# Decays of a selective scan in an SBUF ring of four instead of three PSUM banks

## The reference

```
delta = softplus(d_raw @ dt_proj_w + dt_proj_b)
A = -exp(A_log)
dA  = exp(delta[..., None] * A)                       # the decays
dBx = (delta * xc)[..., None] * Bm[:, :, None, :]     # what is injected
h = dA_t * h + dBx_t                                  # for each token t
y = einsum('bdn,bn->bd', h, c_t)                      # summed over the 16 states
```

## Time and profile before

| what | us |
|---|---|
| median of 3 runs | 1376.31 |
| lowest and highest | 1374.37, 1383.9 |
| profiled execution, first to last instruction | 1379.8 |
| eight scan phases (first to last scan of a batch), together | 480.37 |
| the other stretches behind the first scan, together | 770.85 |

### The profile page before, as it was taken

How to read it: one execution, slowest core, us unless ns; L and a number is a source line. 1 busy time by engine, 2 the same in 40 slices (tenths; PEclk the granted TensorE clock), 3 DMA queues, 4 the chain that set the end, 5 groups by cost and what they waited for, 6 DMA issues and landing times. The chain is left out here.

```text
span 1379.8 us, 19465 instructions
## 1 busy us (share of the span) xinstructions
PE 1207.2 (87%) x6560; PEld 760.5 (55%) x6560; DVE 1037.0 (75%) x2381; ACT 852.2 (62%) x1600; POOL 489.3 (35%) x309
## 2 busy tenths in 40 slices
PE   5974689989998889989999889989899899889698
PEld 3651145655665556555656456655656556555456
DVE  3666977599866997589866997579975998569822
ACT  2634446488646966489565866479664876469332
POOL 0103930078002950069100960049300870029300
PEclk8995579999999999999999999999999999999899
DMA  7101100030001200020001200021000300011000
GB/s 245 70 16 64 60 8 1 16 108 16 16 17 55 69 12 6 16 92 31 17 9 43 88 1 17 16 78 47 16 1 16 109 16 9 1 64 60 8 1 8
DMA packets 18514, 53.22 MB, mean 39 GB/s; under 512 B 4976, under 2 KB 5864, under 8 KB 18032
## 3 DMA queue, kind: packets, MB, share of 16 engines
q1 hardware_dynamic: 16112, 43.40, 9.8%
q0 software_dynamic: 1296, 4.20, 1.0%
q10 hardware_dynamic: 1008, 4.38, 0.8%
HBM read 45.40 MB, written 2.38 MB: 35 GB/s over the span
## 5 line engine op out<-in xcount | busy, mean ns | idle before, releaser
L1482 DVE TENSOR_TENSOR_SCAN probs_T<-bank,probs_T 128x512 f32<-128x512 f32 x256 | 303.9, 1212 | 16.1 <-ACT bank L1078 12.1
L618 PEld LDWEIGHTS bank<-w_w,hidden 128*128 128x128 f32 x2048 | 248.8, 192 | 72.9 <-issue 66.8
L602 PE MATMUL bank<-hT,w_w 128*128 128x512 f32 x512 | 262.9, 629 | 27.1 <-ACT hidden L933 26.2
L447 POOL TENSOR_TENSOR probs_T<-step_space,probs_T 128x1024 f32<-128x1024 f32 x120 | 282.2, 2358 | 5.9 <-DVE probs_T L1482 5.7
L618 PE MATMUL bank<-w_w,hidden 128*128 128x128 f32 x2048 | 251.6, 276 | 2.1 <-DVE expert_sum L1174 1.6
L933 ACT ACTIVATE hidden<-bank,w_b 128x512 f32<-128x512 f32 x256 | 169.6, 686 | 117.5 <-PE bank L602 116.9
L1006 ACT ACTIVATE probs<-bank,row_neg 128x128 f32<-128x128 f32 (+3 forms) x256 | 134.8, 528 | 151.7 <-DVE row_neg L1335 134.8
L1078 ACT ACTIVATE bank<-step_space,a_neg 128x512 f32<-128x512 f32 x256 | 167.8, 683 | 55.0 <-DVE probs_T L1482 36.7
L701 PE MATMUL bank<-k_pad,q_lat 128*128 128x512 f32 (+3 forms) x512 | 185.3, 448 | 5.8 <-DMA k_pad<-xc 5.8
L1335 DVE TENSOR_REDUCE row_neg<-bank 128x1 f32<-128x128 f32 (+3 forms) x256 | 123.5, 487 | 85.1 <-PE bank L703 82.7
L602 PEld LDWEIGHTS bank<-hT,w_w 128*128 128x128 f32 x512 | 89.0, 194 | 153.0 <-ACT hidden L933 97.0
(11 more groups left out here) (183 smaller groups left out, 1577.6 us busy)
## 6 DMA issues: line engine op xcount, KB each, us to landing
probs_T<-b_rows_dram SPq DMA_DIRECT2D x64, 512.0 KB, 3.7
w_w<-in_w_dram ACTq DMA_DIRECT2D x2, 2048.0 KB, 14.0
k_pad<-xc SPq DMA_DIRECT2D x64, 64.0 KB, 2.0
x_in<-in_x_dram POOLq DMA_DIRECT2D x8, 256.0 KB, 3.3
gate<-gate_rows_dram SPq DMA_DIRECT2D x1, 2048.0 KB, 7.0
out_dram<-x_out POOLq DMA_DIRECT2D x7, 256.0 KB, 2.8
step_space<-in_wmod_dram SPq DMA_DIRECT2D x1, 768.0 KB, 5.6
probs_T<-in_wqT_dram SPq DMA_DIRECT2D x1, 512.0 KB, 4.1
```

The costliest lines, as they stand in the source:

```text
L447: ins = nc.gpsimd.tensor_tensor(inject[:, n % 3, :, :], u[:], row.unsqueeze(1).to_broadcast([P, DH, T]), ALU.mult)
L602: mm(hid1_bank(n)[:], w["w1"][:, n // C1, n % C1 * P:(n % C1 + 1) * P], hT[3][:], start=True, stop=True).then_inc(hid1_mm.sem, 1)
L618: ins = mm(to[:, t * P:(t + 1) * P], hidden[:, (e * C1 + c) % (2 * C1), t * P:(t + 1) * P], w["w2"][:, e * C1 + c, :], start=(c == 0), sto ...
L1482: v.tensor_tensor_scan(state[:, n % 2, c, :], decay(DH * n + c)[:], inject[:, n % 3, c, :], 0.0, ALU.mult, ALU.add).then_inc(st_ok.sem, 1)
```

## The change

The decays go to a new SBUF tensor decay_ring with four slots of 128 x 512 (8 KB in each partition). ScalarE waits for scan k - 4 in place of k - 3. The scan takes its first input from the ring. To make room in SBUF the scratch of the dynamic transfers is set to 4096 bytes. Banks 4, 5 and 0 are no longer written by ScalarE during the scan. No instruction is added, removed or moved on any engine.

```diff
+        decay_ring = sb("decay_ring", [P, 4, T])
...
-        DECAY_BANK = (4, 5, 0)
...
         def decay(k):
 
-            return bank[DECAY_BANK[k % 3]]
+            return decay_ring[:, k % 4, :]
...
                 def decays(k):
-                    if k >= 3:
-                        act.wait_ge(st_ok.sem, st_ok.at(b, k - 2))
+                    if k >= 4:
+                        act.wait_ge(st_ok.sem, st_ok.at(b, k - 3))
                     n, c = divmod(k, DH)
-                    f(decay(k)[:], delta[:, c, :], ACT.Exp, scale=a_neg[:, c, n:n + 1]).then_inc(dec_ok.sem, 1)
+                    f(decay(k), delta[:, c, :], ACT.Exp, scale=a_neg[:, c, n:n + 1]).then_inc(dec_ok.sem, 1)
...
-                        v.tensor_tensor_scan(state[:, n % 2, c, :], decay(DH * n + c)[:], inject[:, n % 3, c, :], 0.0,
+                        v.tensor_tensor_scan(state[:, n % 2, c, :], decay(DH * n + c), inject[:, n % 3, c, :], 0.0,
                                              ALU.mult, ALU.add).then_inc(st_ok.sem, 1)
...
-    nc = bacc.Bacc("TRN2", target_bir_lowering=False, num_devices=1)
+    nc = bacc.Bacc("TRN2", target_bir_lowering=False, num_devices=1, dynamic_dma_scratch_size=4096)
```

## The result

| | before | after |
|---|---|---|
| median, us | 1377.55 (4 runs) | 1573.97 (4 runs) |
| lowest and highest, us | 1374.37, 1383.9 | 1566.92, 1576.36 |
| profiled span, us | 1379.8 | 1574.6 |
| eight scan phases together, us | 480.37 | 675.42 |

The ratio after to before is 1.1416, with a 95% interval of 1.1376 to 1.1456: 14% slower. The forecast was 1592 (range 1550 to 1660).

A forecast was written before the change was run, and what follows sets the result against it. VectorE was taken to bound the scan phases, with a fixed chain between them. Eight phases of 87 us against 480.37 us add 215.6 to 1379.8, giving 1595.4, or 1592 us on the median; range 1550 to 1660.

The forecast's parts named there:

- Phases add one for one, the rest is a fixed chain: Eight scan phases, 480.37 us together: longer phases lengthen the total equally; stretches between them stay near 97.8 us.
- Full exclusion, in either order, for a scan too: A scan with two SBUF inputs and a GpSimd product or sum each wait for the other's whole instruction: +215.6 us.
- The sum: Turn-taking scans, products and sums per phase: bare 83.3 us, taken as 87; eight phases add 215.6 us.
- the surcharge: Per scan phase, 87 us taken over 83.3, for scans in a row and turns sometimes left free.
- The handover: Between VectorE and GpSimd turns, the waiting instruction costs 0.13 us less on GpSimd and 0.16 less on VectorE.
- The ring of four: ScalarE may write four decays ahead, not three: at most 12.1 us of scan waits saved, taken as zero.
- The scratch: Smaller scratch for GpSimd's loads and stores of x: any delay falls in idle time, zero.
- The scan's own length: VectorE's scan with both inputs from SBUF, nothing in its way, takes as long as with one from PSUM: zero.
- The decay's write: ScalarE's exponential takes 619 ns into SBUF against 683 into a bank; both hidden, so zero.
- A: Rival: scans take no turns with GpSimd, only 0 to 12.1 us are saved, say 1372 us; chance 0.08.
- B: Rival: GpSimd's long product gives way midway or the wait is one-sided, half the addition, 1484 us; chance 0.05.
- C: Rival: turns, plus TensorE's clock falling in the longer phases, up to +147 us, about half taken: 1662 us; chance 0.13.

The follow-up runs named there:

- ring3_sbuf: The changed kernel with three SBUF decay slots in place of four and the wait for scan k - 3 as before the change: 1571.04 us, ratio 1.1403.
- tiny_pool_sbuf: The changed kernel with GpSimd's inject products and sums of batches 1 to 7 cut to 16 of 512 elements: 1401.28 us, ratio 1.0173 to the kernel before.
- pool_writes_only: The changed kernel with GpSimd's inject products and sums replaced by memsets of the same outputs: 1372.15 us, ratio 0.9947 to the kernel before.
- half_sbuf: The changed kernel with decays of channel half 0 in two SBUF slots and those of half 1 in PSUM banks: 1463.62 us, ratio 1.0623.

## Why the prediction was right

**Phases add one for one, the rest is a fixed chain.** Right: 195.05 us more in the phases, 194.8 in the span, stretches of 97.7 us as before.

**Full exclusion, in either order, for a scan too.** Right. This was the one open step, since no row of before had a scan with two SBUF inputs. It is now shown from four sides: half the scans from PSUM (they alone stay at 1.21 us), GpSimd's work cut away (loss gone), writes only (loss gone), one read (turns again).

The Trainium skill ("SBUF — State Buffer", "Who interferes with whom") also says that a GpSimd instruction which only writes does not contend. The trace agrees: 951 to 955 ns for 120 memsets beside such scans.

**The sum.** Mechanism right, the surcharge too large. The bare sum of turns was 83.3 us for a phase; measured is 84.4. I had taken 87, for two scans in a row and for turns that stay free; a step came to 5.7 us by that and takes 5.38. The 2.6 us too many in eight phases are 20.6 us, where the forecast was 18 us too high. Of the reasons given for the surcharge, the expert additions cost nothing: a step that holds four of them (718.70 to 724.08 in batch 3) also takes 5.38 us, because they have a PSUM input each and lie beside GpSimd's turns.

```profile
718.70 2.20 DVE L1482 TENSOR_TENSOR_SCAN probs_T<-decay_ring,probs_T 128x512 f32<-128x512 f32 x1
720.82 1.09 DVE L1174 SCALAR_TENSOR_TENSOR expert_sum<-bank,gates,expert_sum 128x128 f32<-128x128 f32 x4
```

The other reason does occur, at the end of the phase. There GpSimd has no inject product left and waits for the read product before its sum, so nothing of GpSimd runs beside the last two read products, and they are not covered (VectorE's rows with the start of the full steps, then GpSimd's):

```profile
687.46 3.32 DVE L1482 TENSOR_TENSOR_SCAN probs_T<-decay_ring,probs_T 128x512 f32<-128x512 f32 x2
...
754.12 1.21 DVE L1482 TENSOR_TENSOR_SCAN probs_T<-decay_ring,probs_T 128x512 f32<-128x512 f32 x1
755.25 1.19 DVE L1162 TENSOR_TENSOR probs<-probs_T,bank 128x1024 f32<-128x1024 f32 x1
756.37 3.35 DVE L1482 TENSOR_TENSOR_SCAN probs_T<-decay_ring,probs_T 128x512 f32<-128x512 f32 x2
...
756.52 2.12 POOL L466 TENSOR_TENSOR step_space<-step_space,probs 128x512 f32<-128x512 f32 x1 [2.28 <-DVE probs L1162]
```

In batch 3 the last three scans and their one sum take 6.6 us (755.33 to 761.97), where the bare sum has 4.3. Against that, the twelve full steps before them take 64.6 us (from 690.78, the end of the two scans that start at 687.46, to 755.33), where it has 65.9. So the bare sum has two errors that partly cancel, and that it comes within 1.1 us is in part luck.

**The handover.** It was read from two collisions as 0.13 us saved on GpSimd and 0.16 on VectorE (1.21 - 0.16 is 1.05, and not the 1.06 of the sum, which is 0.3 us in a phase). A step by that is 2 x 1.06 + 2.23 + 1.14 = 5.49 us; measured 5.38. In the timeline above, the first scan and the sum take 2.15 us together (725.19 to 727.34) where 2.20 was due, the second scan 1.08 for 1.06, and the inject product 2.16 for 2.23.

**The ring of four, zero.** Right: ring3_sbuf is no slower, and where turns are absent the waits for a decay stay (15.0 us in 7 waits in tiny_pool_sbuf, 17.0 us in 8 in pool_writes_only). **The scratch, zero.** Right. **The scan's own length, zero.** Right: the shortest scans are 1191 ns, 1194 before.

**The decay's write.** The sign was wrong, harmlessly. From L1069 (619 ns against 683) it looked cheaper into SBUF; the median of the same line went from 691 ns into a bank to 722 into the ring, and the mean from 683 to 716. L1069 has a constant scale and L1078 one per partition, so the two lines differed in more than their output. The write is hidden. In half_sbuf both forms of line 1078 stand in one program, and the one into the ring is the longer too:

```profile
L1078 ACT ACTIVATE decay_ring<-step_space,a_neg x128: 704/715/725, 122.5 to 1364.9; 128x512 f32<-128x512 f32 x128
L1078 ACT ACTIVATE bank<-step_space,a_neg x128: 667/672/692, 123.1 to 1365.5; 128x512 f32<-128x512 f32 x128
```

The Trainium skill ("ScalarE: Activation LUTs", "Step-by-step: what each stage is for") has the write to PSUM as the faster one; the 31 and the 43 ns agree.

**The rivals.** A (no turns) and B (turns in part) are out: products of 3270 ns, a wait of a whole scan. C (TensorE's clock) is out as a cost: the granted clock in the phases did fall, from 0.97 to 0.90 in batch 3, and TensorE's busy time rose from 54.01 to 60.67 us, but it fits in 84.45.

A point not foreseen: scan 1 of each batch now waits for the second product of L445 (9.3 us in 8 waits), since that product is itself held up until scan 0 is done. It is part of the turns and in the sum.

## What to carry to other kernels

Before an operand of a VectorE instruction goes from PSUM to SBUF, count its SBUF inputs. Here the second one made the scan take turns with GpSimd's products, sums and copies, all of which read SBUF, whole instruction for whole instruction. Such a loss shows as longer instructions on both engines and not as idle time, so compare min/median/max of one line, and look for a few accidental collisions in the trace of before: two of them (1.65 and 1.63 us where 1.26 and 0.69 were due) gave a bare sum of 83.3 us for a phase that took 84.4, and the surcharge on top made it worse. What keeps a PSUM input, such as the read products and the expert additions here, is hidden as long as the other engine has a turn to run beside it; the last read products of a phase had none.

## What the runs showed of the hardware

- On GpSimd, for 128 x 1024 fp32 and nothing in the way, a product of two inputs took 2.34 us, a copy 1.04 and a memset 0.95; for 128 x 512 a sum took 1.25 and a copy 0.61. The product of two inputs is more than twice the copy, which I had not expected.
- The same exponential took 31 ns longer into SBUF than into PSUM (722 against 691 in the median, 128 x 512), and 43 ns longer where both stood in one program (715 against 672, half_sbuf).
- Where both engines always had an instruction waiting for the turn (690.78 to 755.33 us in batch 3), they alternated: one scan, one GpSimd instruction. Where GpSimd waited at a semaphore, two scans followed each other (687.46).
